# One core, attention, ternary MLP and top-2 MoE: the router's row transposes move in between the last down products, ScalarE takes all of its copies, and the first tile's weight products are reordered

## What is computed

```python
x = x + xattn(layernorm(x), ctx, Wq, Wkv_expand, Wout)         # 16 heads, causal
x = x + attn(layernorm(x), w_gate, norm_gate, w_down, norm_down)  # int8 x ternary MLP, 2816 wide
x = x + ffn(layernorm(x), rms_weight, router_w, w_gate, w_up, w_down, sw_gate, sw_up, sw_down)

# ffn, the layer around the change
h = rmsnorm(x) * rms_weight
logits = h @ router_w                       # 1024 x 8
probs = softmax(logits); topv, topi = top_k(probs, 2)
moe = sum over the two experts e of topv_e/sum(topv) * (silu(h @ w_gate[e]) * (h @ w_up[e])) @ w_down[e]
sh = silu(h @ sw_gate) * (h @ sw_up) @ sw_down   # one shared expert, 512 wide, for every token
x + moe + sh
```

## Time and profile before

| | us |
|---|---|
| median of 3 runs | 631.88 (631.66 to 632.05) |
| the profiled execution | 631.64 |
| its span, first to last instruction | 629.8 |

### The profile page before, as it was taken

The page is one execution under the profiler, slowest core; times in us unless marked ns, Lnnn a source line. Parts: engine busy times, 40 slices in busy tenths (PEclk is TensorE's granted clock), DMA queues, the critical chain, the costliest instruction groups (busy, mean ns, idle before and its releaser), DMA issues.

```text
span 629.8 us, 10610 instructions
## 1 busy us (share of the span) xinstructions
PE 611.2 (97%) x3624; PEld 477.2 (76%) x3625; DVE 508.6 (81%) x885; ACT 425.9 (68%) x560; POOL 193.5 (31%) x174
## 2 busy tenths in 40 slices
PE   7999999998999999999998999999999999999996
PEld 6778888887887444444556788898988989889775
DVE  5888888888787787989898569688796887969677
ACT  3998888889755989887575357558384573846630
POOL 2345446426000333426930220040330404214052
PEclk9999999999999999999999999999999999999999
DMA  8977776765246997936999658796876968769457
GB/s 336 401 303 301 308 304 241 309 266 200 101 143 259 417 356 265 407 134 250 400 360 425 236 223 294 250 363 247 301 290 236 367 222 329 278 248 350 135 171 272
DMA packets 31070, 177.91 MB, mean 282 GB/s; under 512 B 4064, under 2 KB 4064, under 8 KB 14784
## 3 DMA queue, kind: packets, MB, share of 16 engines
q1 hardware_dynamic: 25536, 158.64, 65.9%
q0 software_dynamic: 5504, 18.88, 8.3%
HBM read 154.30 MB, written 23.20 MB: 282 GB/s over the span
## 4 chain that ended last, share of the span: by engine, by line
PE 65%; ACT 14%; DVE 13%; issue 4%; DMA 3%; POOL 1%; DVEq 0%; POOLq 0%; ACTq 0%
PE BK L2174 11%; PE BK L307 10%; PE BK L1896 4%; PE BK L319 4%; PE BK L2177 4%; PE BK L313 4%; ACT RA L1390 4%; ACT PR L1417 4%; PE BK L314 4%; PE BK L2144 3%; PE BK L1939 3%; PE BK L2132 2%; PE BK L1841 2%; DVE WL L1038 2%; PE BK L2130 2%
## 5 line engine op out<-in xcount | busy, mean ns | idle before, releaser
L2174 PE MATMUL BK<-EX,WH 128*128 128x320 f32 x384 | 99.4, 342 | 0.0
L705 POOL TENSOR_TENSOR WL<-RC,WH 128x2048 fp32r<-128x2048 f32 x7 | 45.5, 6503 | 167.8 <-ACT WH L1598 167.8
L1038 DVE TENSOR_TENSOR WL<-RA,WH 128x2048 fp32r<-128x2048 f32 x40 | 89.4, 2286 | 9.2 <-ACT WH L1598 8.8
L2177 PE MATMUL BK<-EX,WL 128*128 128x160 f32 x336 | 79.2, 236 | 0.0
L1598 ACT ACTIVATE WH<-RA 128x2048 fp32r<-128x2048 f32 x40 | 73.6, 1905 | 0.1
L2174 PEld LDWEIGHTS BK<-EX,WH 128*128 128x128 f32 x384 | 69.2, 189 | 0.0
L2177 PEld LDWEIGHTS BK<-EX,WL 128*128 128x128 f32 x336 | 64.1, 191 | 0.0
L655 POOL TENSOR_TENSOR HB<-HB,ND (+2 forms) x26 | 28.7, 1120 | 100.4 <-DVE BH L922 99.8
L1489 ACT ACTIVATE RA<-RA,RT 128x2048 int16<-128x2048 f32 x22 | 43.8, 1999 | 3.6 <-DMA RA<-wbit 1.8
L1705 ACT ACTIVATE HX<-SR 128x320 fp32r<-128x320 f32 x16 | 7.6, 472 | 57.0 <-DVE SR L1088 57.0
L1896 PE MATMUL BK<-TG,XQ 128*128 128x512 bf16 x192 | 42.4, 379 | 0.1
(11 more groups left out here) (333 smaller groups left out, 1671.6 us busy)
## 6 DMA issues: line engine op xcount, KB each, us to landing
RA<-wbit SPq DMA_DIRECT2D x54, 1024.0 KB, 6.6
RA<-wmoe SPq DMA_DIRECT2D x40, 1024.0 KB, 6.5
RC<-wmoe SPq DMA_DIRECT2D x20, 1024.0 KB, 8.0
rows<-ZERO POOLq DMA_DIRECT2D x40, 256.0 KB, 8.3
XG<-rows SPq DMA_DIRECT2D x10, 512.0 KB, 3.6
rows<-YS SPq DMA_DIRECT2D x9, 512.0 KB, 4.4
RA<-wqk SPq DMA_DIRECT2D x7, 640.0 KB, 8.5
RA<-wo SPq DMA_DIRECT2D x4, 1024.0 KB, 7.3
```

The source lines that it names most:

```text
L705: e.tensor_tensor(WL[2][:, at], RC[5][:, :], WH[2][:, at].bitcast(f32), ALU.subtract).then_inc(free_c[5], 1)
L1038: e.tensor_tensor(WL[m][:, q * RAW:q * RAW + RAW], RC[j][:, :], WH[m][:, q * RAW:q * RAW + RAW].bitcast(f32), ALU.subtract)\
L2174: mm = e.matmul(bank[GBK[f]][:, 0:2 * R], WH[m][:, at], EX[:, k, :, :].rearrange("p a b -> p (a b)"), start=k == 0, stop=k == KD - 1)
L2177: e.matmul(bank[GBK[f]][:, 0:R], WL[m][:, at], EX[:, k, 0, :], start=False, stop=False)
```

## The change

TensorE: `router_t(0)` and `router_t(1)` move ahead of the two last down parts, `router_t(2)` stands behind them. In `tile(0, 0, 0)` a new function `first_products` takes the place of the loop over `highs` and `lows`: first the high weights by the low and the high rows (16 matmuls), then the logits of tiles 0 to 2, `router_t(3)`, the low weights, the logits of tile 3, and then the up product likewise. The number of matmuls and their shapes stay. The transposed rows of tile 2 go to banks 4 and 5 rather than 2 and 3.

ScalarE: copies both halves of all transposed rows, and takes tile 0's high rows and copies ahead of the first two weight splits. VectorE: gives up its three copies, makes tile 0's low rows ahead of the statistics of tile 2, and splits the second half of the gate weights behind the rows of tile 3 rather than ahead of them. The root and the scaling of tile 3's rows on ScalarE stand together, behind both halves of the second weights (`WH[1]`) and ahead of the third (`WH[2]`).

```diff
-HB3 = ((4, 5), (6, 1), (2, 3), (6, 1))
+HB3 = ((4, 5), (6, 1), (4, 5), (6, 1))
...
 # VectorE
-            def router_evac(t):
-                e.wait_ge(s("h3t_pe"), 2 * t)
-                e.tensor_copy(H3T[t][:, 4:8, :], r3(bank[HB3[t][1]], 4)).then_inc(s("h3t_d"), 1)
...
                 if t == NT - 1:
                     split(0, 0, (0,))
                 second_residual(t)
-                if t == NT - 1:
-                    split(0, 0, (1,))
+                if t == NT - 2:
+                    e.wait_ge(s("h3t_a"), 2)
+                    rows_lo(0)
                 e.wait_ge(s("x3"), t + 1)
                 router_rows(t)
-            rows_lo(0)
-            router_evac(1)
-            router_evac(2)
+            split(0, 0, (1,))
             e.wait_ge(s("lg_pe"), 1)
             split(0, 1, (0,))
-            router_evac(3)
             e.wait_ge(s("lg_pe"), 2)
             split(0, 1, (1,))
             split(0, 2, (0,))
...
 # ScalarE
             def router_evac(t):
-                e.wait_ge(s("h3t_pe"), 2 * t - 1)
-                e.activation(H3T[t][:, 0:4, :], r3(bank[HB3[t][0]], 4), ACT.Copy).then_inc(s("h3t_a"), 1)
+                for q in range(2):
+                    if t:
+                        e.wait_ge(s("h3t_pe"), 2 * t + q - 1)
+                    e.activation(H3T[t][:, 4 * q:4 * q + 4, :], r3(bank[HB3[t][q]], 4), ACT.Copy).then_inc(s("h3t_a"), 1)
...
 # TensorE
             e.wait_ge(s("hqt"), 12)
-            for q in range(2):
-                down_part(3, q, 0, KB)
...
             def router_t(t):
                 e.wait_ge(s("h3"), t + 1)
-                if t in (1, 2):
-                    e.wait_ge(s("x3"), t + 2)
+                if t == 1:
+                    e.wait_ge(s("x3"), 3)
+                elif t == 2:
+                    e.wait_ge(s("et_lo"), 3)
+                    e.wait_ge(s("h3t_a"), 2)
                 elif t == 3:
-                    e.wait_ge(s("h3t_a"), 3)
-                    e.wait_ge(s("h3t_d"), 1)
+                    e.wait_ge(s("h3t_a"), 4)
...
             def logits(t):
-                e.wait_ge(s("h3t_a"), t + 2)
-                if t:
-                    e.wait_ge(s("h3t_d"), t)
+                e.wait_ge(s("h3t_a"), 2 * t + 2)
...
+            def high_weights(m, row, ks, first, last):
+                for k in ks:
+                    ins = e.matmul(bank[m], EX[:, k, row, 0:P], WH[m][:, k * FE:k * FE + FE],
+                                   start=first and k == ks[0], stop=last and k == ks[-1])
+                return ins
+
+            def low_weights(m, ks, last):
+                for k in ks:
+                    ins = e.matmul(bank[m], EX[:, k, 0, 0:P], WL[m][:, k * FE:k * FE + FE],
+                                   start=False, stop=last and k == ks[-1])
+                return ins
+
+            def first_products():
+
+                e.wait_ge(s("et_hi"), 3)
+                e.wait_ge(s("et_lo"), 3)
+                e.wait_ge(s("m_hi"), 2)
+                high_weights(0, 1, range(KD), True, False)
+                high_weights(0, 0, range(KD), False, False)
+                for t in range(NT - 1):
+                    logits(t)
+                router_t(NT - 1)
+                for q in range(2):
+                    e.wait_ge(free_c[q], 1)
+                    ins = low_weights(0, range(4 * q, 4 * q + 4), q == 1)
+                ins.then_inc(s("gate_pe"), 2)
+                logits(NT - 1)
+                e.wait_ge(s("m_hi"), 4)
+                high_weights(1, 1, range(KD), True, False)
+                logits_t()
+                high_weights(1, 0, range(KD), False, False)
+                for q in range(2):
+                    e.wait_ge(free_c[2 + q], 1)
+                    ins = low_weights(1, range(4 * q, 4 * q + 4), q == 1)
+                ins.then_inc(s("up_pe"), 4)
...
-            for t in range(NT - 1):
-                router_t(t)
+            router_t(0)
+            down_part(3, 0, 0, KB)
+            router_t(1)
+            down_part(3, 1, 0, KB)
+            router_t(2)
```

More of the change, by code:

```diff
@@ L283, in program @@
                   "rnd", "tern_a", "tern", "g_pe", "silu", "h", "hq", "ht_pe", "hqt", "d_pe", "x3", "sh_last",
-                  "h3", "h3t_pe", "h3t_a", "h3t_d", "lg_pe", "lgs", "lgt_pe", "pos_rd", "top", "e1", "pos_pe", "cnt", "slots", "scat", "pself", "zero",
+                  "h3", "h3t_pe", "h3t_a", "lg_pe", "lgs", "lgt_pe", "pos_rd", "top", "e1", "pos_pe", "cnt", "slots", "scat", "pself", "zero",
                   "dself",
@@ L1629, in _ @@
             router_scale(0)
-            router_rows(1)
-            split(0, None, (0,))
-            router_rows(2)
             def rows_hi(t):
@@ L1656, in routed_hi @@
                 e.activation(EX[:, :, 0, P:R], XT[:, :, :], ACT.Copy).then_inc(s("et_hi"), 1)
+            router_root(1)
+            rows_hi(0)
+            router_evac(0)
+            router_scale(1)
+            split(0, None, (0,))
+            router_root(2)
+            router_evac(1)
+            router_scale(2)
             e.wait_ge(s("d_pe"), 2 * NT)
             split(0, None, (1,), (0,))
-            rows_hi(0)
-            for q in range(2):
-                e.activation(H3T[0][:, 4 * q:4 * q + 4, :], r3(bank[HB3[0][q]], 4), ACT.Copy).then_inc(s("h3t_a"), 1)
+            router_evac(2)
+            split(0, None, (1,), (1,))
             router_root(3)
-            router_evac(1)
-            split(0, None, (1,), (1,))
             router_scale(3)
-            router_evac(2)
             split(0, None, (2,), (0,))
@@ L2045, in routed_rows @@
                     rows_t(q, XG, at)
[L2047 to L2057, removed]
-            tiles_first = []
+            tiles_first = []
+            def high_weights(m, row, ks, first, last):
[30 more added lines that the diff above has]
+                ins.then_inc(s("up_pe"), 4)
             def last_up():
@@ L2077, in tile @@
                 more = n < NS
-                waits(e, ("et_hi", t * 3 + 3), (free_c[0], gi + 1))
+                if n == 0:
+                    first_products()
+                else:
+                    waits(e, ("et_hi", t * 3 + 3), (free_c[0], gi + 1))
                 if not more:
                     waits(e, ("et_lo", t * 3 + 3))
-                for m in range(2):
+                for m in range(2 if n else 0):
                     if m and n == NS - 1:
@@ L2089, in tile @@
                                            for k in range(4 * q, 4 * q + 4)], q == 0)
-                        if n == 0:
-                            routing((m, q))
                     e.wait_ge(s("et_lo"), t * 3 + 3)
@@ L2094, in tile @@
                         .then_inc(s(("gate_pe", "up_pe")[m]), (2, 4)[m])
-                    if n == 0:
-                        routing((m, 2))
                 if n < NS - 1:
```

## The result

The changed kernel took 628.41 us (median of 5 runs, 628.06 to 629.34) against 631.66 us before (5 runs, 630.61 to 632.05) on the same chip: a ratio of 0.9947, 95% interval 0.9935 to 0.9958, so 3.25 us or 0.5% faster. The forecast was 629.0 us with a range of 628.3 to 631.1. One later execution of the kernel before, at 642.93 us with a mean granted clock of 0.922, was slow and is left out of every comparison.

What follows compares the result with a forecast made beforehand. TensorE, 97% busy, bounds the kernel. 2.61 us of waits plus some 0.35 us for fewer changes of kind give 2.96 us, less 0.1 for thin margins: 2.9 off, 629.0 us, range 628.3 to 631.1.

Steps and rivals of the forecast that it cites:

- The bound and the two waits: TensorE, 97% busy, sets the end; its waits of 0.90 us before transposes and 1.71 us before logits would go.
- The walk on TensorE: TensorE's queue from 308.29 us, summed without waits: tile 0's products end at 345.4 rather than 348.37, gaining 2.96 us.
- fewer changes of kind: On TensorE around the logits: fewer switches between kinds of matmul, worth some 0.35 us.
- The margins: New waits between engines are met, thinnest 0.4 us at tile 2's scaling and tile 3's copies; 0.1 us taken off.
- Copies on ScalarE at nothing: Handing VectorE's three copies to ScalarE costs nothing, covered by TensorE's 48 weight matmuls and logits; uncovered, about 0.6 us each.
- The clearing: DMAs clearing rows from ZERO end at 335.6 to 339.0 us, before VectorE's logits copy to HE at 339.6.
- rival 1: Clearing still holds VectorE's logits copy: gain nil at 342.9 (631.9 us), half-way 630.5; chance 0.12.
- Rival 3: Third weights' load lands late, delaying ScalarE's tile 3 copies and logits(3); at 339.6, 2.4 us slower, 634.3; chance 0.06.
- Each microsecond past 340.0 costs one: Price of a late clearing at VectorE's logits copy: 1 us lost per us past 340.0.
- the lower clock: TensorE's clock granted below 1.00 with transposes between down parts would make the forecast wrong; no price given.

Runs made afterwards that it cites:

- e10: Changed kernel with the logits of tiles 0 to 2 put between groups of 8, 4 and 4 high-weight matmuls; 629.34 us, ratio 0.9963.
- e3: Changed kernel with the second half of transposed tiles 1 to 3 copied by VectorE again; 629.89 us, ratio 0.9967.
- e5: Changed kernel with 2 more clearing DMAs of 256 KB each, waited for with the others; 632.85 us, ratio 1.0010.
- e4: Kernel before the change, with the logits copied to their own place, so that copy no longer waits for the clearing DMAs; 631.78 us, ratio 0.9999.
- e6: Changed kernel with the third weights' loads waiting for the last residual, not the last down product, so issued 1.7 us later; 630.46 us, ratio 0.9976.
- e2: Changed kernel with the first tile's products in the old order, the gate weights' second-half split left late; 635.65 us, ratio 1.0054.
- e9: e2 with 16 matmuls of 512 columns, results unread, put into an idle bank ahead of its long wait; 633.26 us, ratio 1.0020.
- e1: Changed kernel with the first tile's products in the old order and the gate weights' second-half split ahead of tile 3's rows; 630.08 us, ratio 0.9971.
- e8: Changed kernel with tile 3's rows scaled behind the first half of the third weights' split, not ahead of it; 632.14 us, ratio 1.0003.

## Why the prediction was right

**The bound and the two waits.** Right. TensorE's two idle stretches, 0.90 and 1.71 us, are both gone, and they are most of the 3.2 us: 2.6 by the view's brackets, 2.9 from start to start, as worked out next.

**The walk on TensorE.** Right, and 0.2 us too high. Forecast 345.4 for the end of tile 0's products, from a start at 308.29; measured 344.98 from 308.08. The term that was off is the 4.8 us for a down part: it is 4.75 from start to start (308.08 to 312.83, 313.70 to 318.45), the same as in the 66 in a row before, so the change to transposes behind it costs nothing that the view shows, while the transposes took 0.80 to 0.87 for 0.84. The prediction split its sum into 2.61 us of waits and 0.35 for fewer changes of kind, and 3.18 - 2.61 would leave 0.57 for these. But the brackets count idleness only from the recorded end of the piece before, which lies behind the point at which the next piece could have started. From start to start, the 16 transposes up to the first wait took 325.34 - 322.53 = 2.81 us for 1.68 of work, and the eight weight matmuls up to the second, of which this line of the kernel before is the first,

```profile
330.03 0.50 PE L313 MATMUL BK<-WH,EX 128*128 128x512 f32 x1
```

took 333.85 - 330.03 = 3.82 for 2.04. The waits were worth 1.13 + 1.78 = 2.9 us, and 0.27 is left for the changes of kind. e10's price agrees: the new order has two changes between weight matmuls and logits fewer, 0.30 us.

**The margins.** Right. Tile 2's scaling was forecast to end at 324.0 against 324.4 (323.5 against 324.07), the third weights' load to land at 333.9 (the split started at 333.5), the copies of tile 3 to end at 337.0 against 337.4 (336.4 against 337.0; e10 shows that this one can shrink to 0.1), the logits' copy to start at 339.6 (339.4), the marks to be ready at 345.4 against 345.8 (345.2 against 345.4). The 0.1 us that I took off for them was not needed.

**Copies on ScalarE at nothing.** Right for ScalarE. What the prediction did not say is that they are worth 1.3 us off VectorE (e3): its walk of VectorE leaves them out, but it priced only their coming and not their going.

**The clearing.** Right that it ends in time: in the changed kernel 2 packets are left for 337 to 340 us,

```profile
q0 software_dynamic: 2, 0.00, 0.3%
```

and the last clearing DMA landed 18.8 us after its issue at 319.4, at 338.2, between the two estimates of 335.6 and 339.0 and 1.2 us ahead of the copy. The rates behind the estimates were too even: a mean rate of 36 packets a us misses the trickle at the end, in e5 by 1.7 us. That the trickle comes from DMA engines that finish unevenly is the prediction's reading; no view here splits the packets by engine. The Trainium skill, "DMA: Bandwidth & Descriptors", section "Queues, rings and completion order", says that an engine takes turns between its queues a packet at a time; the trace agrees in the earlier trace rows (111 and 108 packets), and for the last packets of a queue it gives no rate. That rival 1 would have taken the gain is shown by e5, and that the clearing did not matter before, by e4.

**The other rivals.** Rival 3's mechanism is real, by e6, with 0.55 us of margin. But a long wait costs more than its length: in e5 3.54 us of waiting on TensorE (3.19 and 0.35) cost 4.4 us of time (632.85 against 628.41), and the same holds for e2. "Each microsecond past 340.0 costs one" gives 632.7 for e5's copy at 343.7, close to what was measured, and that is luck: the waits were 0.2 us shorter than the delay past 340.0, the forecast that it starts from was 0.6 too high, and the lower clock took 1.6 us that the rule does not have. The prediction left the lower clock without a price, for want of a row; e2, e5 and e9 give one. Rival 3's long wait, 5.3 us on logits(3), was not run.

## What to carry to other kernels

When the engine that sets the end waits for short chains of other engines, moving the start of the chain ahead of a long piece of its own queue is worth the waits themselves, but only if the work behind is put in the order in which its operands become ready: here each half brought about 1.6 us, and the one with a split left in the wrong place was 0.5% slower than before. Walk every queue that the new order touches with start-to-start durations and write down the margin at each meeting point; a sum made so was within 0.6 us of each time and within 0.2 us of each margin; the margin that hangs on a load was 0.55 us in one execution and 0.06 in another (e10). Count work taken off an engine as well as work put on one, and price a new wait of 3 us on TensorE at more than its length.

## What the runs showed of the hardware that I had not expected

After TensorE had waited 4.17 us (e2) and 3.19 us (e5), the granted clock fell from 1.00 to 0.50, from 2.4 to 1.2 GHz, and the weight matmuls behind ran at half to two thirds of their speed: 2.6 and 1.6 us lost on top of the wait. With the wait of e2 filled by matmuls of no use it stayed at 1.00 and the kernel was 2.4 us faster (635.65 to 633.26). Behind waits of 0.90 and 1.71 us (the kernel before), 1.14 (e1), 1.30 (e6) and, in the profiled run, 2.49 us (e8) it stayed at 1.00.

The page's clock is not to be trusted at the very start. It gives 1.00 for the whole span of the kernel before, but TensorE has no matmul for the first 3.15 us there, and then these lines:

```profile
7.25 1.85 PE L1745 MATMUL BK<-WVH,CTH 128*128 128x512 f32 x4
8.94 1.08 PE L1745 MATMUL BK<-WVH,CTL 128*128 128x512 f32 x4
9.86 1.07 PE L1745 MATMUL BK<-WVL,CTH 128*128 128x512 f32 x4
```

Four matmuls of 512 columns take 1.69 us from start to start (7.25 to 8.94) and the next four 0.92 (8.94 to 9.86). The pace of the first four is that of the lower clock, so "full in the whole span" holds only from about 9 us on.

On TensorE, going from a group of f32r weight matmuls to f32 logits and back costs 0.3 us a round (e10), while going from bf16 down matmuls to f32 transposes shows no cost: 22 of the former take 4.75 us either way.
